# An RWKV recurrence inside a decoder layer: the bonus on the diagonal of the scores, the decay product in the scores' PSUM pair, and a new order of four products

## The reference, cut to what matters

```python
xx = shifted(x) - x
a = tanh((x + xx * maa_x) @ w1).reshape(B, T, 5, 32)
mw, mk, mv, mr, mg = einsum('btfd,fdc->fbtc', a, w2)      # five mixes
xw, xk, xv, xr, xg = (x + xx * (maa_n + m_n) for each n)
r, k, v, g = xr @ Wr.T, xk @ Wk.T, xv @ Wv.T, silu(xg @ Wg.T)
w = time_decay + tanh(xw @ decay_w1) @ decay_w2
# 8 heads of 64; for each token t, with decay d = exp(-exp(w)):
#   y_t = r_t (S + u * k_t v_t^T);   S = d_t * S + k_t v_t^T
yn = (y - mean(y)) * rsqrt(var(y) + EPS)                   # per head
return (yn * gamma + beta) * g @ Wo.T
```

## Time and profile before

| | us |
|---|---|
| median of 3 runs | 974.75 (973.49 to 980.55) |
| the profiled execution | 979.77 |
| its span, first to last instruction | 977.6 |
| TensorE's mean granted clock, as a share of 2.4 GHz | 0.935 |

### The profile page before, as it was taken

The page is one execution under the profiler, slowest core; times in us unless marked ns, Lnnn a source line. Parts: engine busy times, 40 slices in busy tenths (PEclk is TensorE's granted clock), DMA queues, the critical chain, the costliest instruction groups (busy, mean ns, idle before and its releaser), DMA issues.

```text
span 977.6 us, 23429 instructions
## 1 busy us (share of the span) xinstructions
PE 850.1 (87%) x9913; PEld 689.9 (71%) x9930; DVE 764.0 (78%) x1205; ACT 494.8 (51%) x719; POOL 148.7 (15%) x210
## 2 busy tenths in 40 slices
PE   2368789898898988989898989999999976989996
PEld 1267778787787877878778878888888854445553
DVE  4768867878778787787747666988889899899984
ACT  3455254343553435535144334544355346889994
POOL 3000102011020110201010200000000123334331
PEclk9678789899999999999988999999999988999999
DMA  9412101102011020110504033033311421322221
GB/s 221 128 46 64 45 12 60 41 24 87 12 54 47 17 94 13 50 29 14 205 2 158 17 131 102 7 131 129 129 54 74 163 67 44 108 87 97 99 69 40
DMA packets 36968, 72.62 MB, mean 74 GB/s; under 512 B 6466, under 2 KB 7234, under 8 KB 35850
## 3 DMA queue, kind: packets, MB, share of 16 engines
q1 hardware_dynamic: 35754, 68.16, 21.1%
q0 software_dynamic: 1120, 3.10, 1.3%
HBM read 57.63 MB, written 12.58 MB: 72 GB/s over the span
## 4 chain that ended last, share of the span: by engine, by line
PE 39%; DVE 10%; issue 4%; POOL 1%; ACT 1%; DVEq 0%; POOLq 0%; ACTq 0%
PE P L62 5%; PE P L63 4%; PE P L64 4%; PE S L2197 4%; PE P L2187 4%; DVE E L1782 2%; PE S L715 2%; PE S L1643 2%; PE S L1630 1%; PE S L1645 1%; PE S L2174 1%; PE S L1597 1%; PE S L1598 1%; PE S L1602 1%; DVE rec L1788 1%
## 5 line engine op out<-in xcount | busy, mean ns | idle before, releaser
L715 PE MATMUL S<-R,K 64*64 64x32 f32 x3072 | 61.2, 229 | 23.1 <-DVE K L1009 13.0
L715 PEld LDWEIGHTS S<-R,K 64*64 64x64 f32 x3072 | 55.2, 144 | 32.6 <-issue 27.3
L380 POOL TENSOR_TENSOR sm<-sm,mhalf 128x16 f32<-128x16 f32 x8 | 30.6, 3828 | 270.2 <-DVE sm L1056 270.2
L2187 PE MATMUL P<-wq,xqT 128*128 128x512 bf16 x240 | 63.5, 385 | 2.5 <-ACT xqT L2116 1.2
L2197 PE MATMUL S<-wq,hqT 128*128 128x512 bf16 x255 | 60.9, 384 | 5.2 <-ACT hqT L2130 5.2
L963 DVE TENSOR_TENSOR xf<-P,xx 128x1024 f32<-128x1024 f32 x40 | 48.9, 1223 | 17.2 <-PE P L642 17.2
L1006 DVE TENSOR_TENSOR R<-R,D 128x256 f32<-128x256 f32 x96 | 41.4, 431 | 25.5 <-PE S L715 25.4
L1782 DVE TENSOR_SCALAR E<-S,upper 128x2048 f32<-128x2048 f32 x16 | 37.6, 2350 | 24.5 <-PE S L1630 24.3
L1788 DVE RECIPROCAL rec<-S 128x512 f32<-128x512 f32 x16 | 53.6, 3352 | 2.3 <-PE S L1645 2.2
L642 PE MATMUL P<-stack,w2s 98*128 98x256 f32 x160 | 32.5, 335 | 24.5 <-DVE xf L963 11.0
L1456 ACT ACTIVATE E<-E 128x2048 f32<-128x2048 f32 x16 | 30.6, 1914 | 43.7 <-DVE E L1782 43.7
(11 more groups left out here) (289 smaller groups left out, 2751.5 us busy)
## 6 DMA issues: line engine op xcount, KB each, us to landing
wch<-in_wff SPq DMA_DIRECT2D x32, 256.0 KB, 3.2
cwch<-in_wff SPq DMA_DIRECT2D x8, 1024.0 KB, 6.4
xt<-in_x SPq DMA_DIRECT2D x8, 512.0 KB, 5.6
y<-in_x SPq DMA_DIRECT2D x8, 512.0 KB, 3.9
out<-y SPq DMA_DIRECT2D x8, 512.0 KB, 3.7
cxt<-out SPq DMA_DIRECT2D x8, 512.0 KB, 4.3
ct<-in_ctx SPq DMA_DIRECT2D x8, 512.0 KB, 5.3
cxr<-out SPq DMA_DIRECT2D x8, 512.0 KB, 7.0
```

The lines of the kernel that those rows point to most:

```text
L715: mm = pe.matmul(ps[half_rows(side), par, b, k, :], K[head_rows(par), r % 2, at:at + HALF], right_tokens(par, g, side, i), start=True, sto ...
L2187: pe.matmul(Hp[:, cols], xqT[t % 2][:, k, :], w1q[:, k, cols], start=k == 0, stop=False)
```

## The change

Five edits. The bonus is left in 16 unused columns of L (`dg` is now a view of PSUM) and VectorE sets it on the diagonal of `within` by one masked copy between levels 4 and 5 (`place_bonus`, signalled by `diag_ready`); the copy of dg, the product with V on GpSimd and y_front are gone, and ScalarE squares y from PSUM and copies it to SBUF. The decay product wd2 goes to L in place of X2. The narrow product goes ahead of level 5, into X0, its Tanhs into a buffer of its own (a5) and ahead of the second stack copies. TensorE's order becomes ... a, narrow, level 5, level 6, r 0, mix 0, r 1, mix 1, values 0, wd1, values 1, mix 2, wd2 ... On ScalarE the copy of r, the Tanh of aw and the Tanh of g move forward, on VectorE rk, and the shift of the norm goes behind the gate of g. Level 1's masked copy gets another order of its inner axes.

```diff
@@ -94,7 +94,7 @@
     R = sb("R", [P, 2 * NC, T])
-    sb("unused", [P, 2 * NC, T])
+    squares = sb("squares", [P, 2 * NC, T])
@@ -223,7 +222,9 @@
     K_flat = K[:, :, :].rearrange("p s n -> p (s n)")
-    ysq = PY[:, :, :].rearrange("p k t -> p (k t)").rearrange("p (b c) -> p b c", b=2)
+    ysq = squares[:, :, :].rearrange("p g t -> p (g t)").rearrange("p (b c) -> p b c", b=2)
+    dg = L[:, 2 * C - HALF // 2:2 * C - HALF // 2 + 2 * H]
+    diagonal = masks[:, len(LEVELS) - 1:len(LEVELS) + 1, :].rearrange("p n t -> p (n t)")
@@ -371,11 +372,6 @@
             if r is not None:
-                pool.wait_ge(bonus_ready, r + 1)
-                pool.wait_ge(v_ready, r + 1)
-                pool.tensor_tensor(PY[:, :, :].rearrange("p k t -> p (k t)").rearrange("p (g n) -> p g n", n=N),
-                                   V[:, :, :].rearrange("p b (h n) -> p (b h) n", n=N),
-                                   wide(dg[:, :].unsqueeze(2), [P, 2 * H, N]), ALU.mult).then_inc(bonus_v, 1)
@@ -428,24 +424,24 @@
             act.wait_ge(a_tanh, 5 * p + 1)
-            for j in range(4):
+            stack_rows(0, 0)
+            stack_rows(0, 2 * D_MIX)
+            for j in range(1, 4):
                 stack_rows(j, 0)
+            act.wait_ge(a1_done, p + 1)
+            for quarter in range(4):
+                act.activation(a5[0:D_MIX, HALF * quarter:HALF * quarter + HALF],
+                               X0[D_MIX * quarter:D_MIX * quarter + D_MIX, C:C + HALF], ACT.Tanh).then_inc(a_tanh, 1)
...
         def stack_second(p):
-            for j in range(4):
+            for j in range(1, 4):
...
-            act.wait_ge(a1_done, p + 1)
-            act.wait_ge(stacked, 8 * (p + 1))
-            act.wait_ge(a_lo, 4 * p + 1)
-            for quarter in range(4):
-                act.activation(a4[0:D_MIX, HALF * quarter:HALF * quarter + HALF],
-                               X1[D_MIX * quarter:D_MIX * quarter + D_MIX, 2 * T:2 * T + HALF], ACT.Tanh).then_inc(a_tanh, 1)
...
             for at in (0, 2 * D_MIX):
-                act.activation(stack[at:at + D_MIX, 4, :], a4[0:D_MIX, :], ACT.Copy).then_inc(g_stacked, 1)
+                act.activation(stack[at:at + D_MIX, 4, :], a5[0:D_MIX, :], ACT.Copy).then_inc(g_stacked, 1)
@@ -465,7 +461,7 @@
                 return
-            act.wait_ge(A_part, 5 * (r + 1))
+            act.wait_ge(diag_ready, r + 1)
@@ -478,11 +474,6 @@
                 hi(q, 4)
-            if t_:
-                act.wait_ge(bonus_done, r + 1)
-                if r > 0:
-                    act.wait_ge(bonus_v, r)
-                act.activation(dg[:, :], L[:, 0:2 * H], ACT.Copy).then_inc(bonus_ready, 1)
@@ -517,6 +508,9 @@
                 accept_wide(r, 5)
+                if last_levels(q, r):
+                    x["bias_q"](0)
+                accept_wide(r, 6)
@@ -524,37 +518,35 @@
                 split_weight("v")
-            if t_:
-                if last_levels(q, r):
-                    x["bias_q"](0)
-                accept_wide(r, 6)
-            if f:
+            if s_:
+                act.wait_ge(r_done, q + 1)
+                if q > 0:
+                    act.wait_ge(level_half, 2 * STEPS * q)
+                act.activation(R[:, :, :].rearrange("p g t -> p (g t)"), X1[:, :], ACT.Copy).then_inc(r_ready, 1)
+            if f:
+                act.wait_ge(wd1_done, p + 1)
+                if p > 1:
+                    act.wait_ge(wd2_done, p - 1)
+                act.activation(aw[p % 2][:, :], L[:, 0:T], ACT.Tanh).then_inc(aw_ready, 1)
...
             if t_:
-                act.wait_ge(y_ready, r + 1)
-                act.activation(ysq, y[:, :, :], ACT.Square).then_inc(y_squared, 1)
+                act.wait_ge(y_done, r + 1)
+                act.activation(ysq, X2[:, :].rearrange("p (b c) -> p b c", b=2), ACT.Square).then_inc(y_squared, 1)
+                if r > 0:
+                    act.wait_ge(x1_out, 16 * r)
+                act.activation(y[:, :, :].rearrange("p b c -> p (b c)"), X2[:, :], ACT.Copy).then_inc(y_ready, 1)
...
                 split_weight("g")
-            if s_:
-                act.wait_ge(r_done, q + 1)
-                if q > 0:
-                    act.wait_ge(level_half, 2 * STEPS * q)
-                act.activation(R[:, :, :].rearrange("p g t -> p (g t)"), X1[:, :], ACT.Copy).then_inc(r_ready, 1)
...
                 x["normalize"](1)
-            if f:
-                act.wait_ge(wd1_done, p + 1)
-                if p > 1:
-                    act.wait_ge(wd2_done, p - 1)
-                act.activation(aw[p % 2][:, :], L[:, 0:T], ACT.Tanh).then_inc(aw_ready, 1)
@@ -565,7 +557,7 @@
                     act.activation(D[:, 2 * T * k:2 * T * (k + 1)].rearrange("p (b t) -> p b t", b=2),
-                                   X2[:, :].rearrange("p (b k t) -> p k b t", b=2, k=NC)[:, k, :, :], ACT.Exp,
+                                   L[:, :].rearrange("p (b k t) -> p k b t", b=2, k=NC)[:, k, :, :], ACT.Exp,
@@ -594,6 +585,12 @@
                 hi(p, 2)
+            if s_:
+                act.wait_ge(g_done, q + 1)
+                if q > 0:
+                    act.wait_ge(z_gated, q)
+                act.activation(S[:, :, :].rearrange("p k t -> p (k t)"), X0[:, :], ACT.Tanh, scale=0.5).then_inc(g_tanh, 1)
+            if f:
@@ -630,9 +622,13 @@
                     pe.wait_ge(ones_ready, 1)
-                pe.wait_ge(stacked, 8 * p + 5)
+                pe.wait_ge(a_tanh, 5 * (p + 1))
+                pe.wait_ge(stacked, 8 * p + 2)
...
             elif j == 1:
+                pe.wait_ge(stacked, 8 * p + 6)
+                pe.wait_ge(a_lo, 4 * p + 2)
+            elif j == 2:
@@ -690,7 +686,6 @@
                 pe.wait_ge(r_ready, r + 1)
-                pe.wait_ge(bonus_ready, r + 1)
@@ -722,13 +717,12 @@
                 pe.wait_ge(rk_ready, r + 1)
-                if r + 1 < PAIRS:
-                    pe.wait_ge(aw_ready, r + 2)
+                pe.wait_ge(ew_ready, NC * (r + 1))
...
                     for k in range(NC):
-                        mm = pe.matmul(L[:, H * b + 2 * k:H * b + 2 * k + 2], PY[:, k, T * b:T * b + T], usel[:, k, :],
+                        mm = pe.matmul(dg.rearrange("p (a b k) -> p b k a", a=2, b=2)[:, b, k, :], PY[:, k, T * b:T * b + T], usel[:, k, :],
@@ -791,51 +784,42 @@
                 mm.then_inc(a_done, 1)
+                if s_:
+                    pe.wait_ge(k_ready, q + 1)
+                for k in range(NC):
+                    for quarter in range(4):
+                        mm = pe.matmul(X0[D_MIX * quarter:D_MIX * quarter + D_MIX, C:C + HALF], w1[:, k, 4 * D_MIX:5 * D_MIX],
+                                       xf[0][:, k, HALF * quarter:HALF * quarter + HALF], start=k == 0, stop=k == NC - 1)
+                mm.then_inc(a1_done, 1)
...
                 x["q_chunk"](0, 3)
-            if f:
-                pe.wait_ge(a_tanh, 5 * p + 1)
-                for k in range(NC):
-                    for quarter in range(4):
-                        mm = pe.matmul(X1[D_MIX * quarter:D_MIX * quarter + D_MIX, 2 * T:2 * T + HALF], w1[:, k, 4 * D_MIX:5 * D_MIX],
-                                       xf[0][:, k, HALF * quarter:HALF * quarter + HALF], start=k == 0, stop=k == NC - 1)
-                mm.then_inc(a1_done, 1)
...
                 x["k_chunk"](0, 0)
+            if s_:
+                if f:
+                    pe.wait_ge(a_tanh, 5 * p + 1)
+                channel_major("r", X1, 0)
...
                     pe.wait_ge(cload_late, 8 * 16)
+                mix(p, 0, X0)
                 if s_:
-                    pe.wait_ge(k_ready, q + 1)
-                mix(p, 0, X0)
-            if s_:
-                if f:
-                    pe.wait_ge(a_tanh, 5 * (p + 1))
-                channel_major("r", X1, 0)
-            if f:
+                    channel_major("r", X1, 1).then_inc(r_done, 1)
...
             if t_:
-                pe.wait_ge(A_part, 5 * (r + 1))
+                pe.wait_ge(diag_ready, r + 1)
...
                 values(0).then_inc(y_begun, 1)
-            if s_:
+            if s_ and not f:
                 channel_major("r", X1, 1).then_inc(r_done, 1)
-            if t_:
-                pe.wait_ge(y_begun, r + 1)
-                values(1).then_inc(y_done, 1)
...
                 x["k_chunk"](0, 1)
-                x["k_chunk"](0, 2)
-                x["k_chunk"](0, 3)
-                x["sum_weights"]()
-                x["project_bv"]()
-                x["v_rows"](0, 0)
@@ -843,16 +827,24 @@
                 mm.then_inc(wd1_done, 1)
+            if t_:
+                pe.wait_ge(y_begun, r + 1)
+                values(1).then_inc(y_done, 1)
+            if last:
+                x["k_chunk"](0, 2)
+                x["k_chunk"](0, 3)
+                x["sum_weights"]()
+                x["project_bv"]()
+                x["v_rows"](0, 0)
+            if f:
...
             if s_:
-                pe.wait_ge(aw_ready, q + 1)
-                if t_:
```

(41 more changed lines are left out.)

17 lines of the change are left out of this document (5 added, 12 removed).

## The result

| | before | after | ratio |
|---|---|---|---|
| median, first comparison | 974.12 | 936.87 | 0.962 [0.9553, 0.9688] |
| median, second comparison | 977.87 | 937.55 | 0.9601 [0.9556, 0.9646] |
| profiled execution, its span | 979.77, 977.6 | 946.25, 944.4 | |
| profiled execution of the second comparison | | 936.98, 935.1 | |
| granted clock of TensorE | 0.935 | 0.947 (0.956) | |

The account below looks back on a forecast made before the run. TensorE bounds the recurrence turn, with waits and low clock: -6.4 - 2.6 + 1.2 = -7.8 us a turn, -39 over five, -6 first turn, -4 last two, total -49, hence 928 us; range 916 to 954.

Parts of the forecast that it names:

- hi(3)'s new wait: VectorE past mix 4: waits about 1.4 us for ScalarE's third high part, now behind the normalized x.
- the other reading: place_bonus on VectorE: a repeated element doesn't count as a hop, so 1.24 us and not 1.85.
- I count 0: Level 1's reordered masked copy: no effect on time, since VectorE waits after it for TensorE's level 2.
- 6.4 less 1.2: TensorE's idle time per full turn: 6.4 us of waits go, 1.2 us net of new waits come.
- the 0.4 at y's transposes: Chain from y_done to y_scaled: 8.5 us against 8.1 of TensorE's work, so a new wait of 0.4.
- the first low stretch: Low clock after the wait for K in a full turn: costs 1.15 us, of 2.6 for both stretches.
- the sum's step: Full turn: the low-clock stretches leave with the waits ahead of them, worth -2.6 us.
- the first turn: Turn before the first y_front: -6 us, from 1.7, 1.1 and 1.4 of the same waits and low clock.
- The filling turns: Turns before the pipeline is full: held by weight splits on VectorE, so a gain of 0.
- the last turns: Last two turns, without a front: -4 us, from -1.4 (wd2's wait), -1.2 (y_front) and -1.4 (dg and level 1).
- y_front's 1.2 in the drained chain: Last two turns: removing y_front from VectorE shortens the chain by 1.2 us.
- its own chains: Full turn: two chains close behind TensorE, y's transposes to level 0's updates (wait 0.3 to 0.4) and y_done to y_scaled (0.4).

Follow-up runs that it names:

- a_mix_first: The changed kernel with TensorE's old order of mix and r products (mix 0, r 0, mix 1, values 0, r 1): 953.08 us, ratio 0.9777.
- a_gate_back: The changed kernel with g's Tanh on ScalarE and the norm's shift on VectorE in their old places in every turn: 943.27 us, ratio 0.9657.
- b_steps_of_four: The kernel before with only the new order of axes in level 1's masked copy: 983.21 us, ratio 1.0061.
- b_small_product: The kernel before with GpSimd's product of V and dg cut from 1024 to 16 columns: 963.62 us, ratio 0.9871.
- a_first_gate: The changed kernel with g's Tanh in its old place in the first projection turn only: 933.04 us, ratio 0.9567.
- a_squares_first: The changed kernel with y's squares and copy ahead of the split of the q weights in the last projections' turn: 936.93 us, ratio 0.9577.
- after_again: The control: the changed kernel again, unchanged, as partner on the same chip: 937.55 us, ratio 0.9601.

## Why the prediction was right or wrong

**Right.** The bound and its place: what TensorE waited for was most of the gain, and the turn came out at 53.65 against 53.6. Most prices held: place_bonus 1.35 (I took 1.24, though twice the 0.71 of the earlier trace rows is 1.42; the "1.2 to 2.5" is 1.4 to 2.6 by these rows), and 0.5 us ahead of level 6 (0.6); the shift at 1.22; hi(3)'s new wait 1.40 (1.4); ahead of level 1 0.45 to 0.47 (0.3 to 0.4). The clock is 1.00 through the full turns. A repeated element counted as a hopping one would have made place_bonus 1.85; it took 1.35, close to the 1.22 that other VectorE instructions of 128x1024 take here, so the other reading was right. The order of TensorE and ScalarE has its worth as argued: a_mix_first and a_gate_back each give back 1.5 to 1.8 a turn.

**Wrong, level 1's copy.** The step "it may go from 1.30 to 0.71 or ... below nothing it can cost, say, 0.6", and "I count 0". It cost 1.2 in duration, twice the bound. The forecast also spoke of runs of the destination A as if they were those of the whole copy: in the old order only A comes in runs of two, while the source and the mask are read 32 adjacent elements at a time; in the new one none of the three has two adjacent elements. The reason for counting 0 was a fact of before, where VectorE waits behind this copy, and b_steps_of_four shows it to be true there in a full turn. I carried it over to a kernel that I had just given a VectorE 1.4 us late from hi(3), and did not ask again what waits behind the copy. One step fed the other: the new wait of 0.9 is theirs together.

**Wrong, but cancelling.** Idle time fell by 4.5 and not by 5.2 (6.4 less 1.2), which is, to 0.2, the 0.9 ahead of level 3 less the 0.4 at y's transposes that never came. The clock gave 3.3 and not 2.6. So that the turn was right to a tenth is luck: two terms were each off by 0.7, in opposite directions.

**Half right, the first low stretch.** I tied it to the wait of 2.0 for K. In b_small_product both are gone together, and with them 1.6 us between levels 1 and 2, as the sum had it. But the number of low stretches didn't fall: another one stands behind the wait of 0.8 instead, at 0.59, and costs nearly nothing only because it took the place of the wait for dg. In a_gate_back such a wait was followed by a low stretch in one turn and by none in the next, and the turns are equally long. So the sum's step, that a stretch goes with its wait, can't be counted on, and what it costs hangs on the waits behind it; in after all waits over 0.9 had left, and so had both stretches.

**Wrong, the first turn.** "The filling turns are held by weight splits on VectorE: 0." They were held by splits on both engines, and the Tanh of g, moved forward and waiting for its product, was set ahead of ScalarE's. The turn itself gained 5.3 (I said 6; the terms that I named add up to 4.2), and the filling turn lost 2.4 of it by the two traces, where the wait itself grew by 4.1. a_first_gate gives 5.2 back with one condition, 4.5 by the medians.

**Wrong, the last turns.** -4 expected, -1.1 or +2.4 seen. y_front's 1.2 in the drained chain did not come out: in the turn of the last projections the wait of 1.4 for y_front was replaced by one of 1.5 for the scaled y, since the squares stood behind the split of q. Taking that away (a_squares_first) halved the wait and made a new one for V. That turn also holds gaps of TensorE of 3.2 us put down to issue (3.5 in before), which I did not look for and cannot explain. The clock of the last two intervals was 0.91 and 0.90 in before, 0.88 and 0.87 in one execution of after and 0.91 and 0.97 in the other, and this alone makes the forecast's -4 hard to test. What bounds these turns is open.

**The total.** Against the end of the recurrence: 3.1 of the 6.5 us between -49 and -42.5 is the first turn, 2.9 the last ones and 0.5 the full turns. Two of the three are turns that I costed in a clause each, while the full turn had its own chains. By the medians the gain is 37.3, which is 11.7 short of the 49. What the 6.5 leaves of that is that before's trace, from which the gains are counted, lay 5 us above the median of before, and that of after_again at its own (936.98 and 937.55).

## What to carry to other kernels

A cover belongs to the kernel in which it was read: once a change makes an engine late, every "nothing waits for it" further down that engine has to be read again, and here two steps counted apart, at 0 and as a harmless wait, made a wait of 0.9 us a turn. When an instruction is moved forward in an engine's order, look at the turns in which its input isn't there yet, and give those a condition. Gains of moves that clear the same wait do not add: 1.2 and 1.3 us a turn alone made 1.7 together. The cost of a low stretch is not that of its slow matmuls when a wait stands behind them: compare where the next level starts, not the busy time.
